# A group's sum turned and added at its eighth tile instead of its third; the experts' rows stored from the last norm's output

## The reference

```python
def gcn_conv(x, src, dst, w, W, b, n):            # self loops of weight 1 were added
    deg = segment_sum(w, dst, n)
    dinv = where(deg > 0, rsqrt(deg), 0)
    norm = dinv[src] * w * dinv[dst]
    return segment_sum((x @ W)[src] * norm[:, None], dst, n) + b

def gnn(x):
    h = relu(gcn_conv(x, ..., W1, b1))
    h = gcn_conv(h, ..., W2, b2)
    h = (h - h.mean(0)) * rsqrt(h.var(0) + 1e-5) * gamma + beta
    return relu(h + x)

x = x + gnn(layernorm(x))
f = layernorm(x)
p = softmax(f @ gate_w + gate_b)                   # 8 experts
cw = p where it is one of the row's two largest, else 0
x = x + sum_e cw[:, e] * (gelu(f @ W1[e] + b1[e]) @ W2[e] + b2[e])    # 256 -> 512 -> 256
```

## Time and profile before

| | |
|---|---|
| median of 3 runs | 2776.79 us |
| the profiled execution's own time | 2760.07 us |
| its span (first to last instruction) | 2758.3 us |
| mean granted PE clock | 0.826 of full |
| busy PE / PEld / DVE / ACT / POOL | 73 / 51 / 33 / 15 / 62 % |
| DMA over the span | 431 MB, 156 GB/s |

### The profile page before, as it was taken

One profiled execution on the slowest core, in us unless ns is written; L12 is line 12 of the kernel. 1 busy time (PEld: TensorE's weight loads), 2 busy tenths in 40 slices (PEclk: granted clock), 3 DMA queues, 4 the chain that ended last, 5 costly groups with the idle time before them and its releaser, 6 DMA issues.

```text
span 2758.3 us, 29927 instructions
## 1 busy us (share of the span) xinstructions
PE 2008.3 (73%) x8514; PEld 1397.0 (51%) x8515; DVE 899.0 (33%) x2676; ACT 424.7 (15%) x1140; POOL 1699.3 (62%) x1679
## 2 busy tenths in 40 slices
PE   0353249887778886665688888888885473999998
PEld 0251014444445444554445555554554362899997
DVE  7970001111122113342113323232323776333332
ACT  1610000000000000111000000000000465344443
POOL 2887732566656666665765666755665544566665
PEclk6555559988889987878889999998998555999999
DMA  9993013454445443334444545544545313688885
GB/s 321 336 312 101 27 40 124 135 165 152 147 138 168 147 151 103 119 117 119 142 148 143 175 154 170 158 145 141 170 154 186 101 58 129 179 209 207 214 210 137
DMA packets 263529, 431.17 MB, mean 156 GB/s; under 512 B 38800, under 2 KB 147023, under 8 KB 263279
## 3 DMA queue, kind: packets, MB, share of 16 engines
q1 hardware_dynamic: 180591, 253.79, 27.8%
q0 software_dynamic: 81088, 173.80, 23.8%
q10 hardware_dynamic: 1728, 2.13, 0.2%
HBM read 339.36 MB, written 91.16 MB: 156 GB/s over the span
## 4 chain that ended last, share of the span: by engine, by line
another core or an unknown queue 34%; PE 28%; issue 17%; DVE 13%; DMA 3%; ACT 1%; SPq 1%; POOL 1%; DVEq 1%; POOLq 0%; ACTq 0%
PE psum L1508 8%; PE psum L1679 6%; PE psum L1687 6%; PE psum L1554 4%; DVE arena L1122 3%; DMA arena<-pair_weights 1%; DMA out_dram<-ACC 1%; PE psum L1467 1%; SPq L453 1%; PE psum L1670 1%; DVE edge_cols L1214 1%; DVE stats L1220 1%; PE psum L1526 1%; DVE ACC L926 1%
## 5 line engine op out<-in xcount | busy, mean ns | idle before, releaser
L575 POOL DMA_INDIRECT arena<-conv_rows,edge_cols x1120 | 1065.3, 951 | 694.3 <-issue 338.7
L1508 PE MATMUL psum<-arena,X 128*128 128x512 f32 x1568 | 805.7, 636 | 220.5 <-issue 141.4
L1554 PE MATMUL psum<-arena 128*128 128x256 f32 x2240 | 595.3, 399 | 78.2 <-issue 64.8
L1554 PEld LDWEIGHTS psum<-arena 128*128 128x128 f32 x2240 | 447.1, 203 | 271.1 <-issue 218.1
L1508 PEld LDWEIGHTS psum<-arena,X 128*128 128x128 f32 x1568 | 314.6, 202 | 512.8 <-issue 434.4
L1146 DVE TENSOR_TENSOR ACC<-ACC,psum 128x256 f32 x80 | 33.8, 422 | 1037.9 <-remote 441.5
L560 POOL DMA_INDIRECT pair_weights<-scale_b,mean_b x224 | 252.3, 1126 | 116.7 <-issue 67.9
L1122 DVE TENSOR_SCALAR arena<-iota,edge_cols 128x128 f32<-128x128 f32 x1120 | 298.1, 359 | 6.1 <-issue 5.9
L650 POOL DMA_INDIRECT out_dram<-ACC x105 | 166.3, 1583 | 108.9 <-DMA out_dram<-ACC 78.3
L729 ACT ACTIVATE arena<-psum 128x256 f32<-128x256 f32 x80 | 30.4, 380 | 1311.7 <-remote 727.5
L1679 PE MATMUL psum<-ACC,arena 128*128 128x128 f32 x1680 | 208.3, 277 | 0.2 <-DVE ACC L1356 0.2
(11 more groups left out here) (287 smaller groups left out, 1532.4 us busy)
## 6 DMA issues: line engine op xcount, KB each, us to landing
arena<-pair_weights SPq DMA_DIRECT2D x329, 256.0 KB
arena<-in_L_ffn_W_dram SPq DMA_DIRECT2D x113, 512.0 KB, 7.9
pair_weights<-zeros SPq DMA_DIRECT2D x4, 12544.0 KB, 44.2
arena<-conv_rows,edge_cols POOLq DMA_INDIRECT x1120
arena<-pair_weights SPq DMA_DIRECT2D x9, 1792.0 KB
conv_rows<-X SPq DMA_DIRECT2D x14, 896.0 KB
X<-in_x_dram SPq DMA_DIRECT2D x12, 896.0 KB
rows_for_experts<-ACC SPq DMA_DIRECT2D x7, 910.0 KB, 4.2
```

What stands on the lines that cost most here:

```text
L575: pool.indirect_dma_start(G[:, n * D:(n + 1) * D], None, y_tab[layer], bass.IndirectOffsetOnAxis(srcT[:, t:t + 1], 0)).then_inc(gathered[n ...
L1508: ins = m.matmul(bank(6 + c, BW), X[:, t * D + c * P:t * D + (c + 1) * P], table, start=(t == 0), stop=(t == NT - 1))
L1554: ins = m.matmul(bank(2 * (k % 2), D), S[:, n * P:(n + 1) * P], G[:, n * D:(n + 1) * D], start=(j == 0), stop=(j == GT - 1))
```

## The change

In the aggregation the turning moves from tile 2 to tile 7 of the next group. In DVE's loop the addition of group k-1 moves behind the masks of group k+1 and ahead of the `finish` steps of step k; as the masks overwrite those of group k-1, they get a wait of their own for `summed`.

The normed rows are stored to `rows_for_experts` from ACC as soon as ACT has written a chunk, with two DMAs per chunk (one for each half of the features, 512 bytes per row), and the four numbers of `choice` with one DMA of 16 bytes per row after the choice. XN, `expert_rows` and POOL's copies go. `copy_turned` now waits for a chunk's stores before it overwrites the chunk, the last chunk is turned into a buffer of its own (`last_turned`), and DVE waits for all stores before it writes `prob`. The tile numbers of c = 2, 5, 8, 11 go from POOL to ACT, as seven operations of 128x105 each.

```diff
-        XN = late(2 * CH * DX)
+        last_turned = late(CH * D)
-        SUM_TURN = 2
+        SUM_TURN = 7
@@ SP, in the loop over the chunks of the output
                         sp.dma_start(out[(NT - 1) * P:N, :], X[0:TAIL, t0:t0 + D]).then_inc(total_set, 16)
-
-                for c in range(NCH):
-                    sp.wait_ge(xn_ready, CH * (c + 1))
-                    sp.wait_ge(choice_in, c + 1)
-                    r0 = (c % 2) * CH * DX
-                    sp.dma_start(rows_of(rows_x, c), tile3(XN[:, r0:r0 + CH * DX])).then_inc(xn_stored[c % 2], 16)
+                    sp.wait_ge(n_ready, CH * (c + 1))
+                    for k in range(KC):
+                        sp.dma_start(rows_of(rows_x, c)[:, :, k * P:(k + 1) * P],
+                                     tile3(acc[:, k, c * CH * P:(c + 1) * CH * P])).then_inc(xn_stored[c % 2], 16)
+                sp.wait_ge(choice_set, 1)
+                sp.dma_start(rows_x[0:NP, D:DX].rearrange("(t p) d -> p t d", p=P), tile3(choice, NT)).then_inc(choice_in, 16)
@@ POOL
-                pool.wait_ge(choice_set, 1)
-                for c in range(NCH):
-                    if c >= 2:
-                        pool.wait_ge(xn_stored[c % 2], 16 * (c // 2))
-                    g.tensor_copy(tile3(XN[:, (c % 2) * CH * DX:(c % 2 + 1) * CH * DX])[:, :, D:DX],
-                                  choice[:, 4 * CH * c:4 * CH * (c + 1)].rearrange("p (t k) -> p t k", k=4)
-                                  ).then_inc(choice_in, 1)
-
                 pool.wait_ge(choice_set, 2)
...
-                for c in range(2 * NCH):
-                    if c % HOTS == 0:
-                        continue
+                for c in range(1, 2 * NCH, HOTS):
...
-                    pool.wait_ge(xn_stored[n], 16 * SLOT_CH[n])
+                    pool.wait_ge(xn_stored[n], 32 * SLOT_CH[n])
+                pool.wait_ge(choice_in, 16)
@@ ACT
                 def copy_turned(c):
+                    act.wait_ge(xn_stored[c % 2], 32 * (c // 2 + 1))
...
-                def expert_rows(c):
...
                 def places(c):
                     _, at, node = hot_parts(c)
                     act.wait_ge(hot_at, c + 1)
-                    a.activation(node[:, :, 0], at.rearrange("p n t -> p t n"), ACT.Copy,
-                                 scale=place[:, 0:1]).then_inc(hot_place, 1)
-
-                for c in range(NCH - 2):
-                    expert_rows(c)
+                    ins = a.activation(node[:, :, 0], at.rearrange("p n t -> p t n"), ACT.Copy, scale=place[:, 0:1])
+                    if c % HOTS == 2:
+                        for t in range(CH):
+                            ins = a.activation(node[:, t, 1], at[:, :, t], ACT.Copy, scale=float(c % NCH * CH + t + 1))
+                    ins.then_inc(hot_place, 1)
+
                 for c in range(2 * NCH):
                     places(c)
-                    if c in (2, 5):
-                        expert_rows(NCH - 2 + c // 3)
@@ DVE, aggregate
                             if k + 1 < GG:
+                                if k:
+                                    dve.wait_ge(summed, GG * layer + k)
                                 build(k + 1)
...
+                            if k:
+                                add_group(k - 1)
                             if layer == 1 and k and 0 in FINISH[1][1][k - 1]:
                                 set_shift(chain_fast)
                             for i in FINISH[layer][1][k]:
                                 finish(layer, i)
-                            add_group(k)
+                        add_group(GG - 1)
@@ DVE, after the norm
-                    v.tensor_copy(acc[:, :, q * P:(q + 1) * P], turned(j).rearrange("p (c n) -> p c n", c=KC)
-                                  ).then_inc(n_copied, 1)
+                    v.tensor_copy(last_turned[:, j * D:(j + 1) * D], turned(j)).then_inc(n_copied, 1)
                 dve.wait_ge(logit_done, 1)
+                for n in range(2):
+                    dve.wait_ge(xn_stored[n], 32 * SLOT_CH[n])
@@ PE
                 def gate(q):
                     pe.wait_ge(n_copied, q + 1)
+                    at = (q - (NCH - 1) * CH) * D
                     for k in range(KC):
-                        m.matmul(bank(2, T8)[:, q * NX:(q + 1) * NX], acc[:, k, q * P:(q + 1) * P],
+                        rows = acc[:, k, q * P:(q + 1) * P] if at < 0 else last_turned[:, at + k * P:at + (k + 1) * P]
+                        m.matmul(bank(2, T8)[:, q * NX:(q + 1) * NX], rows,
...
-                    if c % HOTS:
-                        pe.wait_ge(hot_tile, c - c // HOTS)
+                    if c % HOTS == 1:
+                        pe.wait_ge(hot_tile, c // HOTS + 1)
```

More of the change, by code:

```diff
@@ L277, in gnn_ffn @@
         member_set, rank_done = sem("member_set"), sem("rank_done")
-        xn_ready, choice_set, choice_in = sem("xn_ready"), sem("choice_set"), sem("choice_in")
+        choice_set, choice_in = sem("choice_set"), sem("choice_in")
         xn_stored = [sem(f"xn_stored{n}") for n in range(2)]
```

## The result

The changed kernel takes 2800.8 us (median of 9 runs, 2795.81 to 2811.18) against 2775.86 us (9 runs, 2761.2 to 2789.46) for the kernel before: a ratio of 1.0098, 95% interval 1.007 to 1.0125. It is slower by 25 us where 13 us less were forecast, and it lies outside the range of 2735 to 2790. The profiled execution took 2798.79 us, 2 us under its median; that of the kernel before, 2760.07, lies 15.8 us under its own, so the two traces stand further apart (38.7 us) than the medians.

What follows compares the result with a forecast made beforehand. The prediction took POOL's gather stream and its pauses in the two aggregations (845 and 843 of 2758 us) as the bound. Terms -4 - 3 + 1 - 9.5 + 2.5 = -13 us took the median 2776.79 to 2764, range 2735 to 2790.

Steps and rivals of the forecast that it cites:

- The aggregation, -4 us: Turning at tile 7: a tenth of the 43 us that POOL's waits longer than 2.9 us offer, -4 us.
- PE's third linear map stands for a `finish` behind the addition: Aggregation, tile 8, steps with three or four maps: PE stops 1 to 2 us, inside 6.9 us of slack in layer 0.
- a turning seen up to 24 us late: Aggregation: PE's completions are announced up to 24 us late while POOL streams gathers; no mechanism was given.
- The starved-groups rival: Aggregation: turning at tile 7 is seen too late for the next group's start; 56 us lost, 2824 us, chance 0.13.
- Pauses gone: Aggregation rival: PE going on readies sums sooner, so POOL's 2.9 us pauses go; -44 us, 2720 us, chance 0.16.
- End of layer 1, -3: Last group, no gather behind it: PE's 5.55 us wait for the copy is filled with tiles, -3 us.
- Norm stores, +1: Stores from the norm: ACT's copy-back waits for the sixth chunk's stores, some 5.3 us, +1 us.
- Choice: Storing the choice in one DMA of 6272 16-byte pieces: covered by 58 us before the first gather, zero.
- Slots and POOL beside DVE, -9.5 + 2.5 = -7: Slot stage: earlier expert list, ACT setting the pace, -9.5 us; POOL's list slowing DVE's places, +2.5 us.

Runs made afterwards that it cites:

- u3: Changed kernel with u2's waits, and z2's wait at the additions of groups 26, 29, 32, 35 alone: 2477.13 us.
- z3: Changed kernel with z2's wait, but the `finish` steps ahead of the wait and the addition: 2425.9 us.
- z2: Changed kernel; in layer 0, k = 27 to 38, DVE adds group k-1 only when the gathers of group k+1 have landed: 2532.29 us.
- u2: Kernel before; in layer 0's groups 27 to 38, ACT's copy of sum k and POOL's group k+2 wait for group k+1's gathers to land: 2450.13 us.
- y1: The changed kernel as it is, measured again in a later session: 2417.17 us against 2425.22 for the kernel before.
- z1: The kernel before, unchanged, measured and traced again in a later session: 2425.34 us.
- x4: Changed kernel with DVE's addition of group k-1 behind the `finish` steps of step k instead of ahead of them: 2415.91 us.
- u4: u3 with the `finish` steps of step k ahead of the late addition: 2440.35 us.

## Why the prediction was wrong

**The aggregation, -4 us, is the term that failed.** It was +47.7. Within it the step that the runs show is this one, and it holds for layer 0's 29.3 us: PE's third linear map stands for a `finish` behind the addition, "1 to 2 us, inside its 6.9 us of slack". The place was right and the size was not: the stop was 13 us once and 20 to 22 us three times in the changed kernel's first trace, and the three long ones cost 9 to 10.5 us each (10.3, 9.1 and 10.5 at groups 30, 33, 36; 9.1 to 9.4 in u3). The other 18.4 us, in layer 1, have no step of the prediction that a run names. The prediction had the other factor two paragraphs earlier, a turning seen up to 24 us late, and used it for the next group's start alone. The slack was also misread: PE has 6.9 us at tile 2 because the announcement ends that wait, so moving PE on doesn't carry the slack to tile 8. (This reading is argued from the two timelines; no run tests it alone.)

**The starved-groups rival** (0.13) had the sign and the origin, a turning at tile 7 announced late, and not the place. It said that PE waits at the start of group k+2. z3 has exactly these waits and loses 9.5 us once; z2, where only the order of `finish` and addition differs, loses about 9.7 us in every group.

**"Pauses gone"** came true in half, as the three pauses of 12.6 us took their place. The short pauses that remain in the changed kernel's trace, at groups 30, 33, 36 and 39, are still 2.75 to 2.84 us long though PE no longer stands at its turnings (3.5 us in all for 70.9), which bears out that they hung on POOL's own stream and not on PE. u2 gives their price, 28 us; as it has the pause built in, it says nothing on their cause.

**End of layer 1, -3:** PE's wait at the last turning was 2.05 us for 5.55, -3.5 us; it is part of the 47.7. **Norm stores, +1:** 0.95 us, before the sixth chunk alone, as said; on another chip ACT's last copy-back came 1.6 us later (109.4 us behind the last copy of a sum in y1, 107.8 in z1). The fourteen stores landed in 3.2 to 5.6 us, 4.6 in the middle; 5.3 was the estimate. **Choice:** no wait of POOL for it stands ahead of the first expert gather (4.39 us for DVE), so 0 holds. The DMA of 6272 pieces of 16 bytes landed 10.7 us after its issue (10.1 to 10.9 in three other traces): just the 11 us that the prediction took as the lower bound from the price of 512-byte pieces, far from the 58 us that were there. So the small pieces cost no more each than the large ones. **Slots and POOL beside DVE, -9.5 + 2.5 = -7:** measured -11.5 + 0.4 = -11.1. ACT's group of seven took 1.88 us (estimated 2.5) and wasn't the pace; DVE was, at 6.07 us for three steps against the estimated 6.9. The list beside DVE's places cost 0.4, not 2.5. The conflict of DVE and POOL was looked for in the list, where it was small, and not in the slot steps, where taking it away gave 4.4 us of the gain.

Where PE's counts are in time, the whole sum of -13 measured -8.

**Still open:** why PE's counts come late behind POOL's indirect DMAs in one measurement and not on four chips; and layer 1's 18.4 us. The order of x4 wasn't measured where counts are late by themselves. By u4 it should be the better one there, and it is equal to the change elsewhere (2414 to 2416 for 2417 us).

## What to carry to other kernels

On an in-order engine, ask of every wait not only what it costs but who waits for the work behind it: put the work that frees another engine's buffer ahead of a wait for something that may be late. A wait moved later isn't made harmless by slack seen at its old place; if the slack was made by the same late signal, it doesn't move along. And measure a change of a per cent more than once, on more than one chip, before it is believed: here the sign differs between the first measurement and the later ones.

## What was not expected of the hardware

One kernel took 2776 us in one measurement and 2422 to 2426 us on four chips. In the first trace DVE, ACT and POOL see PE's counts up to 24 us after PE's record while POOL issues indirect DMAs in the aggregation. In the first stage it is more. DVE's copies of the turned rows show it, and PE's own records beside them (both of the kernel before, first trace):

```profile
325.49 1.29 DVE L1114 COPY ACC<-psum 128x512 f32<-128x512 f32 x2 [54.71 <-remote]
391.29 1.29 DVE L1114 COPY ACC<-psum 128x512 f32<-128x512 f32 x2 [64.51 <-remote]
...
242.81 1.01 PE L1508 MATMUL psum<-arena,X 128*128 128x512 f32 x1 [1.79 <-issue]
245.61 1.01 PE L1508 MATMUL psum<-arena,X 128*128 128x512 f32 x1 [1.79 <-issue]
```

PE's record of the fifth set of transposes ends at 237.48 and that of the sixth at 304.78; DVE copies them at 325.49 and 391.29, 88.0 and 86.5 us later. The changed kernel's first trace has the same 88.0 and 86.5 us; in z1 the copy follows by 0.1 us. And the late count isn't all: from 240 to 397 us PE's matmuls stand alone, mostly 2.8 us apart, behind no wait that the profile shows, where z1 does twelve of them in 5.3 us beside the same stream of POOL. So in the first measurement PE's own work was slow too, and "late announcements" is a name for one sign of that state. Stages without such a stream take the same time in both (612 and 614 us). The cause isn't known.
